# Gate and info convolution of a two-block fp32 network: nine taps on four row tiles of TensorE in place of three taps on shifted planes

## What is computed

```python
x  = _conv(attn, o_w, 0) + x                       # x1 in the kernel
xn = _ln_last(x, ln2_g, ln2_b)                     # LayerNorm over the last axis (W)
gate = gelu(_conv(_conv(xn, g1, 0), g3, 1))        # 32 -> 64 channels, 3x3, zero padding
info =      _conv(_conv(xn, i1, 0), i3, 1)         # 32 -> 64 channels, 3x3, zero padding
out = _conv(gate * info, r1, 0) + x                # x2 in the kernel, input of block L1
```

## Time and profile before

| | us |
|---|---|
| median of 3 timed runs | 289.95 |
| lowest and highest | 288.15, 292.16 |
| profiled execution, first to last instruction (span) | 286.2 |
| PE busy in it | 222.9 (78%) |
| VectorE busy | 189.8 (66%) |
| ScalarE busy | 129.2 (45%) |
| GpSimd busy | 75.9 (27%) |

### The profile page before, as it was taken

The page is one execution under the profiler, slowest core; times in us unless marked ns, Lnnn a source line. Parts: engine busy times, 40 slices in busy tenths (PEclk is TensorE's granted clock), DMA queues, the critical chain, the costliest instruction groups (busy, mean ns, idle before and its releaser), DMA issues.

```text
span 286.2 us, 4575 instructions
## 1 busy us (share of the span) xinstructions
PE 222.9 (78%) x1738; PEld 143.5 (50%) x1738; DVE 189.8 (66%) x417; ACT 129.2 (45%) x256; POOL 75.9 (27%) x56
## 2 busy tenths in 40 slices
PE   0429868999669997798999986998529989368963
PEld 0229518824229734654589255745115536136843
DVE  5595365527596768999747974835999738882532
ACT  2230142234383355549822565429347557444440
POOL 3928204004004302540045125000464300304150
PEclk9999997999979999799999997999859999779987
DMA  7210011000011000000000200000000000000101
GB/s 198 53 46 2 0 40 53 0 2 0 1 55 37 2 0 1 2 0 21 0 2 0 73 3 1 2 0 2 0 37 3 0 0 3 0 0 3 39 0 39
DMA packets 3654, 5.17 MB, mean 18 GB/s; under 512 B 1136, under 2 KB 1872, under 8 KB 3632
## 3 DMA queue, kind: packets, MB, share of 16 engines
q1 hardware_dynamic: 3392, 4.29, 5.0%
q10 hardware_dynamic: 240, 0.58, 0.6%
HBM read 3.30 MB, written 1.05 MB: 15 GB/s over the span
## 4 chain that ended last, share of the span: by engine, by line
PE 64%; DVE 17%; ACT 10%; issue 5%; DMA 2%; SPq 0%; ACTq 0%; DVEq 0%
PE ps L1132 16%; PE ps L1186 15%; PE ps L1143 8%; PE ps L1278 6%; PE ps L1302 5%; PE ps L1222 4%; ACT sh_ln L467 4%; ACT p_t L560 3%; DVE sh_in L278 3%; DVE sh_ln L278 2%; DMA w3b<-in_w_gi 2%; PE ps L1262 2%; PE ps L1112 2%; DVE q_bd L933 1%; DVE xm L922 1%
## 5 line engine op out<-in xcount | busy, mean ns | idle before, releaser
L1132 PE MATMUL ps<-w_qk,sh_ln 128*128 128x128 f32 x192 | 46.9, 409 | 11.6 <-DVE sh_ln L278 7.8
L376 POOL TENSOR_TENSOR ln_s<-ln_s,neg_half 128x16 f32<-128x16 f32 x8 | 23.3, 2910 | 112.6 <-DVE ln_s L726 112.6
L1132 PEld LDWEIGHTS ps<-w_qk,sh_ln 128*128 128x128 f32 x192 | 45.6, 330 | 14.3 <-issue 14.3
L1186 PE MATMUL ps<-sh_ln,w_gi 96*128 96x512 f32 x96 | 42.4, 596 | 0.5 <-ACT v L484 0.5
L1222 PE MATMUL ps<-sh_in,w_in 128*32 128x256 f32 x384 | 25.6, 424 | 10.6 <-DVE sh_in L278 10.6
L467 ACT ACTIVATE sh_ln<-ln_out 32x496 f32<-32x496 f32 (+1 forms) x44 | 27.2, 618 | 11.6 <-DVE ln_out L737 11.0
L278 DVE COPY sh_ln<-ln_out 32x496 f32<-32x496 f32 (+2 forms) x60 | 28.0, 466 | 3.4 <-PE ps L1143 2.4
L1186 PEld LDWEIGHTS ps<-sh_ln,w_gi 96*128 96x128 f32 x96 | 17.9, 190 | 22.1 <-issue 21.9
L1222 PEld LDWEIGHTS ps<-sh_in,w_in 128*32 128x32 f32 x384 | 13.3, 123 | 23.3 <-DVE sh_in L278 10.8
L1143 PE MATMUL ps<-sh_ln,w_v 128*32 128x512 f32 x96 | 22.4, 1077 | 0.0
L829 DVE TENSOR_TENSOR gi<-ps,gate 64x512 f32<-64x512 f32 x16 | 11.1, 694 | 13.9 <-ACT gate L498 13.5
(11 more groups left out here) (125 smaller groups left out, 336.5 us busy)
## 6 DMA issues: line engine op xcount, KB each, us to landing
x_norm<-in_x SPq DMA_DIRECT2D x4, 256.0 KB, 2.8
x_res<-in_x SPq DMA_DIRECT2D x4, 256.0 KB, 2.5
out_x<-out_s SPq DMA_DIRECT2D x4, 256.0 KB, 2.0
sh_ln<-ln_out SPq DMA_DIRECT2D x8, 64.0 KB, 2.0
kc<-in_shape_consts ACTq DMA_DIRECT2D x1, 450.0 KB, 5.8
w3b<-in_w_gi SPq DMA_DIRECT2D x1, 288.0 KB, 6.3
vec<-in_vectors SPq DMA_DIRECT2D x1, 131.5 KB, 3.3
w3a<-in_w_qkv ACTq DMA_DIRECT2D x1, 108.0 KB, 3.3
```

Of the source, the lines that this page charges most:

```text
L376: nc.gpsimd.tensor_tensor(ln_s[n][:, 3, :], ln_s[n][:, 2, :], neg_half[:, :], ALU.pow)\
L1132: mm = nc.tensor.matmul(to, sh_ln1[:, i, at:at + D * P - D + 1:D], w_qk[:, dy, :, :, :].rearrange("p d m c -> p (d m c)"), start=(dy == 0) ...
L1186: mm = nc.tensor.matmul(ps[:, GI_BANKS[2 * i + h], :], w_gi[:, dy, :, :].rearrange("p m o -> p (m o)"), xs[:, i, y:y + H // 2, 0:W], start ...
```

## The change

`ln2_out` becomes a bordered image block: 10 rows of 34 columns for each block of 8 rows of 32. DVE's last LN2 operation writes the inner part. The border columns stay zero from the memset; the row above and below each block come from the neighbouring partition block by two DMAs of SyncE's queue (`ln2_edges`, 96 partitions x 2 x 34 elements each), for which the new signal `g_edge` stands. `sh_ln2`, its memset and the twelve plane copies of a pair are gone. `w_gi` holds the nine taps, repeated on the four partition blocks; the fold on PE has 24 matmuls in place of 6, in banks 5 to 7, and DVE copies three times in place of once. `qk(0, 1)` no longer waits for the gate and info fold.

`gate_info` now does both images at once: four row tiles, each with 32 rows of contraction (the partition block r) and 128 columns, nine taps of 512 columns each, every row tile into its own bank. This makes 36 matmuls, 72 instructions a pair, in the order dy, dx, r, the middle row (dy = 1) first; `g_i` is incremented by the last tap of each row tile. A bank now holds block r of both images. `reduce_1` reads `gi` accordingly. In the tail the whole `gate_info(last)` stands before `window_q`. The orders on ACT and DVE are otherwise as they were.

```diff
-        w_gi = sb("w_gi", [3 * C, 3, 2, EC])
+        w_gi = sb("w_gi", [P, 3, 3, 2, EC])
-        ln2_out = sb("ln2_out", [P, 2, BLK])
+        ln2_out = sb("ln2_out", [P, 2, RH + 2, PW])
-        sh_ln2 = sb("sh_ln2", [3 * C, 2, PLANE])
+        g_edge = signal("ln2_edges", 32, start=1)
...
+            def ln2_edges(pair):
+                alone(sp)
+                sp.wait_ge(g_ln[1].sem, g_ln[1].done(pair))
+                sp.dma_start(ln2_out[C:P, :, 0, :], ln2_out[0:P - C, :, RH, :]).then_inc(g_edge.sem, 16)
+                sp.dma_start(ln2_out[0:P - C, :, RH + 1, :], ln2_out[C:P, :, 1, :]).then_inc(g_edge.sem, 16)
@@ sync: step
                 load_res(pair + 2)
+                ln2_edges(pair + 1)
                 if norm:
                     ln1_planes(pair + 3)
@@ sync: around the steps
             load_res(1)
+            ln2_edges(0)
             ln1_planes(2)
...
+            ln2_edges(last)
             store(but_last)
@@ gpsimd
-            clear(sh_ln2)
+            clear(ln2_out)
@@ scalar: step (and the same for pair 0 and for the last)
                 v4_evac(pair + 2)
-                ln2_planes(pair + 1)
                 tanh_mask(pair)
@@ vector: other_constants
-                gi_f = ps[0:3 * C, 1, 0:6 * EC].rearrange("p (m y o) -> p m y o", m=2, o=EC)
-                nc.vector.tensor_copy(w_gi[:, :, :, :].rearrange("p y m o -> p m y o"), gi_f).then_inc(s_wready, 1)
+                for s in range(3):
+                    gi_f = ps[:, 5 + s, 0:6 * EC].rearrange("p (m y o) -> p m y o", m=2, o=EC)
+                    nc.vector.tensor_copy(w_gi[:, :, s, :, :].rearrange("p y m o -> p m y o"), gi_f)\
+                      .then_inc(s_wready, 1)
@@ vector: ln_apply
+                if name == "ln2":
+                    dve.wait_ge(g_i.sem, g_i.before(pair))
+                    dve.wait_ge(g_edge.sem, g_edge.before(pair))
+                    image = [t.rearrange("p (i y) x -> p i y x", i=2)
+                             for t in (ln_per_col(2 * n + 1), ln_d[n][:, :, :])]
+                    nc.vector.tensor_tensor(dst[:, :, 1:1 + RH, 1:1 + W], image[0], image[1], ALU.subtract)\
+                      .then_inc(g.sem, 1)
+                    return
@@ vector: ln2_apply
                 ln_apply(1, ln2_out, "ln2", pair)
-                planes("ln2", ln2_out, sh_ln2, g_ln[1], g_i, pair)
@@ tensor: fold
                 for s in range(3):
-                    mm = nc.tensor.matmul(ps[C * s:C * s + C, 1, 3 * EC * m:3 * EC * m + 3 * EC],
-                                          w1b[:, C * m:C * m + C], w3b[:, s, m, :], start=True, stop=True)
+                    for r in range(R):
+                        mm = nc.tensor.matmul(ps[C * r:C * r + C, 5 + s, 3 * EC * m:3 * EC * m + 3 * EC],
+                                              w1b[:, C * m:C * m + C], w3b[:, s, m, :], start=True, stop=True)
@@ tensor
-            def gate_info(pair, i):
-                xs = plane(sh_ln2)
-                planes_ready("ln2", pair)
-                pe.wait_ge(g_x1.sem, g_x1.done(pair))
-                for h in range(2):
-                    for dy in range(3):
-                        y = H // 2 * h + dy
-                        mm = nc.tensor.matmul(ps[:, GI_BANKS[2 * i + h], :],
-                                              w_gi[:, dy, :, :].rearrange("p m o -> p (m o)"),
-                                              xs[:, i, y:y + H // 2, 0:W], start=(dy == 0), stop=(dy == 2))
-                    mm.then_inc(g_i.sem, 1)
+            def gate_info(pair):
+                pe.wait_ge(g_ln[1].sem, g_ln[1].done(pair))
+                for dy in (1, 0, 2):
+                    if dy == 0:
+                        pe.wait_ge(g_edge.sem, g_edge.done(pair))
+                    for dx in range(3):
+                        for r in range(R):
+                            rows = slice(C * r, C * r + C)
+                            mm = nc.tensor.matmul(ps[:, GI_BANKS[r], :],
+                                                  w_gi[rows, dy, dx, :, :].rearrange("p m o -> p (m o)"),
+                                                  ln2_out[rows, :, dy:dy + RH, dx:dx + W],
+                                                  start=(dy == 1 and dx == 0), stop=(dy == 2 and dx == 2))
+                            if dy == 2 and dx == 2:
+                                mm.then_inc(g_i.sem, 1)
@@ reduce_1
-                    mm = nc.tensor.matmul(ps[C * r:C * r + C, 1, :], w_r1[:, r // 2, :],
-                                          gi[:, :, BLK * (r % 2):BLK * (r % 2) + BLK], start=True, stop=True)
+                    mm = nc.tensor.matmul(ps[C * r:C * r + C, 1, :], w_r1[:, r % 2, :], gi[:, r // 2, :],
+                                          start=True, stop=True)
@@ tail
-            gate_info(last, 0)
+            gate_info(last)
             window_q(but_last)
             window_k(but_last)
-            gate_info(last, 1)
             reduce_1(last)
```

More of the change, by code:

```diff
@@ L192, in build @@
                          for e in (("dma",) if n == "ln1" else ()) + ("dve", "act")}
-                     for n in ("ln1", "ln2", "x2", "in")}
+                     for n in ("ln1", "x2", "in")}
+        g_edge = signal("ln2_edges", 32, start=1)
         g_qkt = signal("qkt_in_psum", 2)
@@ L284, in build @@
         Z_LN1, Z_LN2, Z_X2, Z_IN, Z_PADS = 3, 4, 5, 6, 7
-        W_QKV, W_ALL = 3, 8
+        W_QKV, W_ALL = 3, 10
         @block.sync
@@ L571, in ln1_planes @@
                 planes("ln1", ln1_out, sh_ln1, g_ln[0], g_v4, pair)
-            def ln2_planes(pair):
-                planes("ln2", ln2_out, sh_ln2, g_ln[1], g_i, pair)
             def x2_planes(pair):
@@ L624, in _ @@
             act.wait_ge(s_zero, Z_PADS)
-            ln2_planes(0)
             v4_evac(1)
@@ L644, in _ @@
             in_planes(but_last)
-            ln2_planes(last)
             tanh_mask(but_last)
@@ L1324, in step @@
                 window_v(pair)
-                gate_info(pair + 1, 0)
-                gate_info(pair + 1, 1)
+                gate_info(pair + 1)
                 probs_transposed(pair)
@@ L1332, in _ @@
             qk(0, 0)
-            pe.wait_ge(s_fold, 2)
-            pe.wait_ge(s_wready, W_QKV + 1)
             qk(0, 1)
@@ L1348, in _ @@
             pe.wait_ge(s_diag, 16 * (1 + R + 2))
-            gate_info(0, 0)
-            gate_info(0, 1)
+            gate_info(0)
             reduce_1(0)
```

## The result

| | before | after |
|---|---|---|
| median of the runs, us | 289.88 (20 runs: 288.15 to 292.75, and one of 494.62) | 291.21 (20 runs, 289.61 to 293.12) |
| profiled execution: span, us | 286.2 | 287.7 |
| its mean granted clock | 0.937 | 0.914 |

The kernel after takes 1.006 times the time of the kernel before (95% interval 1.0034 to 1.0087): 0.6% slower, some 1.3 us in the medians and 1.5 us in the spans. gate_info became shorter by 2.5 us or more in each of its four places, and in the sum nothing of it arrives at the end. (A ratio here leaves disturbed runs out on both sides, a median doesn't, so the two can differ a little.)

A forecast was written before the change was run, and what follows sets the result against it. No engine bounds it all: PE has 64% of the chain, and DVE or ACT chains set its waits. Start -1.3, pair 0 +0.2, steps +3.3 and -1.9, tail +0.8: +1.1 on 289.95, so 291.0 us; range 286 to 300.

The forecast's parts named there:

- pace of gate_info: PE's gate_info: 72 instructions on four row tiles side by side take 7.9 us a pair, a gain of 2.6.
- start: Kernel start: POOL's smaller memset ends sooner, so DVE's first plane copy and all behind it come 1.3 us sooner.
- pair 0: First gate_info: shorter matmuls but later gelus and products, -0.5, and reduce_1 at lower clock, +0.7; together +0.2 us.
- step of pair 0: ACT's LN1 copies between the gelus delay window_out, +1.9, and PE's idle gap costs clock, +1.4; together +3.3 us.
- step of pair 1: No LN1 copies there, so window_out starts at 194.2 against 196.10: -1.9 us, no clock charged for the gap.
- tail: Last gate_info: reduce_1 0.6 us sooner, but the scores lose clock after PE's idle gap, +1.4; together +0.8 us.
- the rival of a worse pace: gate_info's row tiles run slower than a quarter; at 0.129 us an instruction +5.7, so 296.7 us; chance 0.22.
- Removed copies: In both steps, ACT's tanh and DVE's next product come sooner without the LN2 plane copies; gate_info starts 1.0 us sooner.
- Edge DMAs: Two issues a pair on SP's queue, with 22 us of cover in a step before gate_info: cost 0.
- the further fold work: 18 more fold matmuls at the start, done while PE waits for the planes; no cost charged.
- the two more copies of the weights: Two more DVE copies of folded weights, 1.1 us, covered by PE's first qk: cost 0, without cover 1.1.
- the rule read off `window_out`: PE gaps near 3 us or more cost clock, pair 1's 2.4 us does not; window_out took 3.15 us after 2.24.

The follow-up runs named there:

- the two experiments: Changed kernel plus dummy copies into an unread spare tile: five on ACT ahead of the tanh, 291.2 us; or seven on DVE behind LN2's last product, 290.6 us.
- the kernel with the copies last: Changed kernel with ACT's six LN1 plane copies of pair 3 moved from between the gelus to behind the x2 plane copies: 286.5 us, ratio to before 0.992.
- the one with the DVE copies: Changed kernel plus seven DVE copies of ones into an unread spare tile behind LN2's last product: 290.6 us, ratio to before 1.007.
- the one with the early table load: Changed kernel with ACT's LN1 copies ahead of gelu 0 and a one-element Gelu before them: 289.2 us, ratio to before 0.9995.
- the fillers: Unused matmuls on constants in PE's waits before reduce_1; alone on the changed kernel (5, 2, 3) 287.2 us, in two combined kernels 285.4 and 285.2 us.
- the three of ACT's order: Changed kernel with LN1 copies ahead of gelu 0, 291.0 us; the same with gelu's table loaded early, 289.2; copies behind the x2 plane copies, 286.5.

## Why the prediction was right, point by point

The time, 291.0, and the sign of the span's change (+1.1 predicted, +1.5 measured) came out. The parts, from the starts of the same stretches in the chains of the two profiled executions, one of each kernel:

| | predicted | measured | from |
|---|---|---|---|
| pace of gate_info, us a pair | 7.9 | 7.98 | chain, 72 instructions |
| start | -1.3 | -1.16 | first qk 19.62, 18.46 |
| pair 0 | +0.2 | +0.11 | gate_info to the step's qk: 22.16, 22.27 |
| step of pair 0 | +3.3 | +2.2 | 58.84, 61.07 |
| step of pair 1 | -1.9 | -0.95 | to attn_out: 55.01, 54.06 |
| tail | +0.8 | +1.25 | the rest: 86.95, 88.2 |

*Pace.* Right, and the rival of a worse pace fell. The Trainium skill ("TensorE: Matmul & The Clock Gate", "Measured speedup vs the span model") gives 3.07x for this tiling. Here it is 31.5 / 7.98 = 3.95x, with the prediction's 31.5 us (72 x 0.438) for one tile after the other, and the measurement decides.

*Start.* Right in mechanism and size.

*Removed copies.* gate_info starts 37.15 us after the step's qk against 38.18, so 1.03 us sooner (predicted 1.0), and by the two experiments ACT's copies, not DVE's, are what it hung on: five shorter ones brought back 0.51 us of it, DVE's none.

*Edge DMAs, the further fold work, the two more copies of the weights.* Costed at nothing, and nothing is seen.

*Step of pair 0.* The mechanism was right and the size was off in both terms. `window_out` starts 16.74 us after gate_info's start, against 13.73 before; the prediction had 16.6. Of this ACT's queue gives 16.24 (its evacuations end at 137.76), which with the 1.03 us is +1.5 and not +1.9; the last 0.5 us are `reduce_1` at half clock. That and 0.25 us of `window_out` are all that followed the 5.84 us of idle PE here, 0.75 us and not 1.4: the granted clock of `window_out` was 0.89. One sentence of the step was a misreading: that the LN1 copies were ready long before. Placed ahead of the gelus, they showed that their input comes 2 us before gate_info ends. The trace of the kernel before has it already: DVE writes `ln_out` from 128.83 to 129.52, and the copies start at 129.58.

*Step of pair 1.* The step that failed is the rule read off `window_out`, that a wait of 2.2 to 2.4 us costs no clock and one near 3 does. The wait was 2.53 us and `reduce_1` and `window_out` took 0.88 and 0.39 us longer behind it. Without them this step would have been at -2.2. In the kernel with the copies last the same wait cost nothing, and the step came out at -1.9 against before. The two errors, 1.1 us too much in one step and 0.95 too little in the other, cancel; that the total came out so well is luck.

*Tail.* Behind gate_info, 13.71 us to `reduce_1` against 14.08, so -0.4 (predicted -0.6), then 6.85 us to the last conv1 against 5.34, so +1.5 (predicted +1.4, the clock). Not foreseen: mask_conv and conv2 took 7.57 us in place of 6.88, at clock 0.70 and not 0.78; their wait was the same 6.3 us, and nothing of the change touches them. The end gave 0.4 us back, in which the last mask_conv was 0.2 us faster.

*Pair 0.* The conv1 behind the wait was at full clock this time (2.78 us, 4.07 before), after `reduce_1` (1.54, 1.07 before) and attn_out (2.07, 1.13 before) had taken the slow part. The 1.3 us bought nothing: the next qk waited for ACT's LN1 planes, 2.34 us in place of 1.06.

So where did 10 us of shorter matmuls go? Four row tiles finish together, so gelus, products and evacuations that had run under the later matmuls now run behind all of them. Of the 2.5 us each, this leaves 0.4 us in pair 0, 1.2 us in the step of pair 1 (clock left out) and 0.4 us in the tail, and in the step of pair 0, where the LN1 copies stand between, it takes 2.5 us more than was gained. The kernel with the copies last shows that this excess is order: there ACT's evacuations end 12.53 us after gate_info's start and not 16.31 us, and `window_out` starts 134.81 - 121.58 = 13.23 us after it in the timeline, half a microsecond less than before the change. With `reduce_1` at half clock, as in the kernel after, it would have been 0.9 us later, an estimate. Splitting gate_info by image, so that the first half could be evacuated early, wasn't tried: PE would write a bank that ACT reads, and what that costs no run shows.

## What to carry to other kernels

Before making a matmul on the path faster by packing tiles, write down what its consumers did while it ran: packed tiles end together, and the saving is only what remains after the evacuation chain has come out from under the matmuls. Then go through the queue of the engine that does this chain, and put work whose reader is far away behind it; here that was worth 1.4%, part of it clock, with a move of two lines, while the packing alone lost 0.6%. And keep the tile index innermost, since nearly all the overlap is gone if one tile is finished before the next begins.

## What the runs showed of the hardware that was not expected

The length of PE's wait does not decide by itself whether the clock drops. `reduce_1` took 1.94 us after a wait of 2.53 us, and 1.06 us after one of 3.31 us with the copies last; in the tail, behind 3.40 us, it took 1.73 and 1.78 us in these two kernels, and 1.13 us in the one with the DVE copies. The scores of the step of pair 0 started after a wait of 2.41 or 2.42 us in every kernel. They ran at clock 0.70 in the kernel after, and at 1.00 in the one with the early table load, where the first 32 took 1.90 us in place of 2.65: the same code, from the scores to gate_info, took 7.50 us in one execution and 6.01 us in the other. Windows of the kernel after, then of that one (this one begins 1.6 us ahead of the scores):

```profile
113.95:119.70 5.75, 5.75 (x70) 5.02 (x72) 5.22 (x5) 2.45 (x13) 3.34 (x3) 0.70 0.02 3
```

```profile
112.00:117.60 5.60, 4.04 (x65) 3.56 (x67) 5.43 (x6) 3.65 (x19) 4.10 (x3) 1.00 0.02 4
```

Such drops go with the spread of the runs: over 35 runs of the kernel before, spans went from 285.9 to 291.4 us, and the longer ones had the lower mean clock (correlation -0.75). What in a given execution decides on a drop stays open. What the traces count is this: with the fillers, `reduce_1` took 1.06 or 1.07 us in all nine places (three kernels, three places each), and in only 3 of 18 such places without them (the kernel after, the three of ACT's order and the two with copies put back).

Also not expected: PE that was busy without a pause, but on one row tile of 32 rows, fell to a granted clock of 0.50. In the four gate_infos with the tiles in turn this came 2, 3, 6 and 4 us after their start, and the clock stayed there until their end (0.85 us for each instruction of 512 columns); in the kernel after, four such tiles beside each other took 0.11 us an instruction.
